# A fused attention and mixture-of-experts block: the last four batches of phase one in an order of their own, padding rows written during the steps, gates chosen in the expert stage

## The reference

```python
h = _layernorm(x) * (1 + ca) + sa
x = x + ga * attention(h)      # linear attention: 16 heads of 8, cumulative sums over the 256 tokens
h = _layernorm(x) * (1 + cb) + sb
x = x + gb * ffn(h)
# ffn: h = rmsnorm(h @ W_in.T); logits = h @ Wr.T; the best 2 of 8 experts by logits + bias
#      gates = softmax of the two chosen logits
#      expert e: rmsnorm((silu(h @ Wg[e].T) * (h @ Wu[e].T)) @ Wd[e].T)   (512 hidden)
#      out = sum of gates * expert outputs; rmsnorm(out) @ W_out.T
```

## Time and profile before

| | |
|---|---|
| median of 3 runs | 432.0 us (431.47, 432.0, 436.98) |
| profiled execution | 440.27 us, of which the span of the profile is 438.4 us |
| granted TensorE clock over the span | 0.931 of full |
| busy share of the span | PE 84%, DVE 77%, ACT 66%, POOL 57% |
| phase one, steps with all stages | about 30 to 180 us |
| drain, table, first loads | about 180 to 228 us |
| expert stage | about 228 to 398 us |
| last stage | about 403 to 438 us |

### The profile page before, as it was taken

The page is one execution under the profiler, slowest core; times in us unless marked ns, Lnnn a source line. Parts: engine busy times, 40 slices in busy tenths (PEclk is TensorE's granted clock), DMA queues, the critical chain, the costliest instruction groups (busy, mean ns, idle before and its releaser), DMA issues.

```text
span 438.4 us, 13203 instructions
## 1 busy us (share of the span) xinstructions
PE 366.1 (84%) x3906; PEld 321.1 (73%) x3907; DVE 338.8 (77%) x1113; ACT 290.9 (66%) x814; POOL 249.9 (57%) x221
## 2 busy tenths in 40 slices
PE   4799999979999999873129999999999999991464
PEld 3588878768888888762118999999999999981353
DVE  5077898869999998665599887878788788781586
ACT  4425768867888887534427776877768587773585
POOL 2964476668888888833532545456455554555341
PEclk9989999999999999985559999999999999998588
DMA  8994000000000000000141222122221222112933
GB/s 252 428 356 190 2 18 20 20 21 26 24 27 28 24 30 24 32 26 24 50 151 38 61 64 72 48 72 56 64 68 53 66 54 73 37 38 63 372 85 96
DMA packets 19107, 35.67 MB, mean 81 GB/s; under 512 B 3843, under 2 KB 14614, under 8 KB 18294
## 3 DMA queue, kind: packets, MB, share of 16 engines
q1 hardware_dynamic: 14262, 21.20, 15.4%
q0 software_dynamic: 4544, 9.39, 6.4%
q10 hardware_dynamic: 272, 4.72, 2.8%
HBM read 23.80 MB, written 13.47 MB: 85 GB/s over the span
## 4 chain that ended last, share of the span: by engine, by line
PE 56%; DVE 19%; issue 10%; DMA 7%; ACT 3%; POOL 3%; DVEq 1%; another core or an unknown queue 0%; ACTq 0%; SPq 0%; POOLq 0%
PE bank L1518 8%; PE bank L1520 8%; PE bank L1519 8%; PE bank L1335 6%; DVE prod L890 5%; PE bank L1533 4%; PE bank L1535 4%; PE bank L1534 4%; DMA gates_bc<-gate_rows 3%; PE bank L1504 2%; PE bank L1417 2%; DVE st L813 2%; PE bank L1444 1%; ACT junk L782 1%; DVE x_all L1085 1%
## 5 line engine op out<-in xcount | busy, mean ns | idle before, releaser
L543 POOL DMA_INDIRECT expert_rows<-late,to_place x78 | 86.7, 1111 | 83.2 <-DVE late L1191 56.8
L524 POOL DMA_INDIRECT dispatched<-rows,pos x64 | 67.1, 1049 | 38.0 <-issue 19.1
L1518 PE MATMUL bank<-late,w_hi 128*128 128x256 f16 x312 | 85.8, 275 | 1.5 <-issue 0.6
L1519 PE MATMUL bank<-late,w_hi 128*128 128x256 f16 x312 | 85.6, 274 | 0.0
L1520 PE MATMUL bank<-late,w_lo 128*128 128x256 f16 x312 | 85.6, 274 | 0.0
L506 POOL TENSOR_TENSOR kv<-kv,v 128x1024 f32<-128x1024 f32 x32 | 67.6, 2132 | 21.6 <-ACT kv L643 14.8
L1335 PE MATMUL bank<-cst,kv 128*128 128x128 f32 x576 | 77.0, 286 | 1.2 <-POOL kv L506 1.0
L1335 PEld LDWEIGHTS bank<-cst,kv 128*128 128x128 f32 x576 | 72.0, 201 | 1.9 <-POOL kv L506 1.1
L1180 DVE SCALAR_TENSOR_TENSOR kv<-bank,uscale,kv 128x512 f32<-128x512 f32 x78 | 58.0, 746 | 19.2 <-ACT kv L729 13.9
L729 ACT ACTIVATE kv<-bank,descale 128x512 f32<-128x512 f32 x78 | 53.5, 687 | 27.6 <-PE bank L1520 26.8
L735 ACT ACTIVATE kv<-kv 128x512 f16<-128x512 f32 x78 | 49.2, 631 | 20.5 <-DVE kv L1180 18.6
(11 more groups left out here) (212 smaller groups left out, 797.1 us busy)
## 6 DMA issues: line engine op xcount, KB each, us to landing
late<-dispatched SPq DMA_DIRECT2D x39, 129.0 KB
late<-wguT ACTq DMA_DIRECT2D x1, 4096.0 KB, 15.8
late<-expert_rows SPq DMA_DIRECT2D x1, 2064.0 KB, 11.2
gates_bc<-gate_rows SPq DMA_DIRECT2D x1, 2048.0 KB, 15.1
wd<-wdT SPq DMA_DIRECT2D x1, 2048.0 KB, 23.8
out<-kv SPq DMA_DIRECT2D x16, 128.0 KB, 1.8
expert_rows<-late,to_place POOLq DMA_INDIRECT x78
late<-expert_rows SPq DMA_DIRECT2D x1, 1032.0 KB, 6.8
```

Of the source, the lines that this page charges most:

```text
L524: pool.indirect_dma_start(hbuf, bass.IndirectOffsetOnAxis(ap=pos[:, p, t * K + k:t * K + k + 1], axis=0), rows[:, p, t, k, :], None).then_ ...
L543: pool.indirect_dma_start(ybuf, bass.IndirectOffsetOnAxis(ap=to_place[:, s, r:r + 1], axis=0), yt[:, s, r, :], None).then_inc(y_scat[s], 16)
L1518: mm(o, w_hi[:, w], hi, start=True, stop=False)
L1519: mm(o, w_hi[:, w], lo, start=False, stop=False)
```

## The change

Three things are changed.

1. Steps 17 to 20 are replaced by a `drain` function on PE, DVE, ACT and POOL, with an order of its own on each engine. To let batches overlap, odd batches use another PSUM bank (`UL_ODD` in KV's bank) for the expert features, ranks of b13 to b15 go to `LAST_RANK`, logits no longer wait for ACT's upper half, and ACT's upper half waits for the logits (`lr_done`). The scales of the down weights are computed in 6 DVE instructions in place of 9.
2. The filler rows are written in phase one: SP issues 17 DMAs of 2048 rows of 516 bytes (256 rows in each of the 8 regions), the whole of `dispatched`, two in flight. `positions` on DVE waits until the filler under the rows that the batch can reach has landed. The eight DMAs after the last batch, and `tail`, go.
3. The choice of the gates' logits moves from before L1148 into the third tile of the expert stage, and ACT's sigmoids to the end of that stage.

```diff
-            for s in range(B, B + 5):
-                step(*(at(s - g) for g in stages))
+            step(*(at(B - g) for g in stages))
+            drain(*(at(B - 4 + g) for g in range(4)))
...
-            sp.wait_ge(tail_done, 1)
...
-                sp.dma_start(hbuf[bass.ds(row, R), :], filler[e * R:(e + 1) * R, :]).then_inc(filled, 16)
+            sp.wait_ge(x_rest, 48)
+            sp.wait_ge(moe_ld, 32)
+            regions = hbuf[0:E * REGION, :].rearrange("(e r) w -> r e w", e=E)
+            padding = filler[0:E * R, :].rearrange("(e r) w -> r e w", e=E)
+            for s in range(REGION // R):
+                if s >= 2:
+                    sp.wait_ge(padded[s % 2], 16 * (s // 2))
+                sp.dma_start(regions[s * R:(s + 1) * R], padding).then_inc(padded[s % 2], 16)
...
             def positions(b, p, n):
                 dve.wait_ge(ohs_done, b + 1)
+                dve.wait_ge(padded[p], 16 * n)
...
# ScalarE
+            def drain(b12, b13, b14, b15):
+                last_rows(*b12)
+                spread(*b14)
+                turned_back(*b14)
+                second_turned(*b13)
...
+                squares(*b13, UL_ODD)
+                second_deviation(*b14)
+                last_rows(*b13)
+                spread(*b15)
+                second_norm(*b14)
...
# VectorE
+            def choice(b, p, n):
+                ul = UL_ODD if p else UL
+                dve.wait_ge(rms_done, b + 1)
+                nc.vector.reciprocal(rrs[:, p, :], rms[:, p, :]).then_inc(rrs_done, 1)
+                dve.wait_ge(rrs_done, b + 1)
+                logits(b, p, ul if b > B - 4 else UL)
+                scores(b, p, ebias[:])
...
+            def drain(b12, b13, b14, b15):
...
+                choice(*b13)
+                second_inverse(*b14)
+                second_shift(*b14)
+                denominators(*b15)
+                best_two(*b13)
+                rows_low(*b13)
+                slots_of(*b13)
+                quotients(*b15)
+                count_chosen(*b13[0:2])
+                add_attention(*b15)
+                choice(*b14)
+                second_inverse(*b15)
+                second_shift(*b15)
+                best_two(*b14)
+                rows_low(*b14)
+                slots_of(*b14)
+                count_chosen(*b14[0:2])
+                projection_scales()
+                choice(*b15)
+                best_two(*b15)
+                rows_low(*b15)
+                slots_of(*b15)
+                count_chosen(*b15[0:2])
...
-            then(nc.vector.tensor_tensor(tail_f[:], total[0:1, :], cst[0:1, C_REG:C_REG + E], ALU.add))
-            nc.vector.tensor_copy(tail[:], tail_f[:]).then_inc(tail_done, 1)
+            then(nc.vector.tensor_copy(total[:], TOTAL))
...
                     low_part(t, s, i, 0)
+                    if first and s == 2:
+                        choose_gates()
...
# TensorE
+            def drain(b12, b13, b14, b15):
+                running_state(b15, 0, False)
...
+                spread(*b14)
+                turn(*b13)
+                running_state(b15, 1, False, range(1))
+                ranks(*b12)
+                running_state(b15, 1, False, range(1, 3))
+                head_sums(b15, 0)
+                project(*b14)
+                into_experts(*b13)
+                head_sums(b15, 1)
+                spread(*b15)
+                ranks(*b13)
+                turn(*b14)
+                into_experts(*b14)
+                project(*b15)
+                ranks(*b14)
+                turn(*b15)
+                into_experts(*b15)
+                ranks(*b15)
```

More of the change, by code:

```diff
@@ L526, in step, with drain @@
                                 rows[:, p, t, k, :], None).then_inc(scattered[p], 16)
-            pipelined(pool, step)
+            def drain(*batches):
+                for rte in batches:
+                    step(None, None, None, None, None, rte)
+            pipelined(pool, step, drain)
             pool.wait_ge(w_small, 2)
@@ L587, in norm, with rows_high @@
                 last.then_inc(done, 1)
+            def rows_high(b, p, n, ul=UL):
+                if again(n):
+                    act.wait_ge(scattered[p], 16 * NT * K * (n - 1))
+                nc.scalar.activation(rows[:, p, :, :, D:HW].rearrange("p t k o -> p (t k) o"),
+                                     place_sb[:, bass.ds(b * NT * K, NT * K)].unsqueeze(2), ACT.Copy)
+                for t in range(NT):
+                    last = nc.scalar.activation(
+                        rows16[:, p, t, :, 0:D], ul[:, t, 0:D].unsqueeze(1).to_broadcast([P, K, D]),
+                        ACT.Copy, scale=rrs[:, p, t:t + 1])
+                last.then_inc(hi_done, 1)
@@ new lines, in squares @@
+            def squares(b, p, n, ul=UL):
+                act.wait_ge(u_ps, b + 1)
+                for t in range(NT):
+                    last = nc.scalar.activation(junk[:], ul[:, t, 0:D], ACT.Square, accum_out=ssq[:, p, t:t + 1])
+                    last.then_inc(ssq_done, 1)
+                    act.wait_ge(ssq_done, NT * b + t + 1)
+                nc.scalar.activation(rms[:, p, :], ssq[:, p, :], ACT.Sqrt, bias=eps_rms_h[:],
+                                     scale=1.0 / D / HSCALE ** 2).then_inc(rms_done, 1)
@@ L601, in step @@
-                    last.then_inc(hi_done, 1)
+                    act.wait_ge(rrs_done, rte[0] + 1)
+                    rows_high(*rte)
                 if prj is not None:
[L603 to L606, removed]
+                    spread(*prj)
                 if nrm is not None:
@@ L704, in projection_high @@
                                      scale=wd_by[:]).then_inc(wdhi_done, 1)
[L706 to L708 removed]
+            pipelined(act, step, drain)
+            for c in range(DN):
                 projection_high(c)
[L712 to L722 removed]
             def gate(t, s, i, h):
@@ L1483, in _ @@
+            pipelined(pe, step, drain)
             pe.wait_ge(count_done, B)
-            mm(bk[0][:, 0:E], ones16[:], oh_all[:, B, NT * K, :], start=True, stop=True).then_inc(total_ps, 1)
+            mm(TOTAL, ones16[:], oh_all[:, B, NT * K, :], start=True, stop=True).then_inc(total_ps, 1)
             pe.wait_ge(table_done, 1)
```

292 lines of the change are left out of this document (185 added, 107 removed).

## The result

The changed kernel is slower: 468.3 us (median of 4 runs, 464.2 to 473.3) against 434.0 (431.5 to 437.0) for the kernel before beside it, a ratio of 1.076 with a 95% interval of 1.063 to 1.088. The run of 473.3 was in a slower state, with a lower granted clock, and isn't in the ratio. Its profiled execution took 464.2 us, with a span of 462.1.

What follows compares the result with a forecast made beforehand. PE was taken to be full outside the drain and handover. Drain 7.7 plus gates and landing 1.7 less added waits 0.5 made 8.9 us, off the median of 432.0: 423.1 us, range 419 to 430.5 (forecast's own 420.5 to 426).

Steps and rivals of the forecast that it cites:

- What bounds the kernel: PE bounds the expert stage, PE and DVE phase one's full steps; only the 46.8 us of drain and handover can shorten.
- Part 1, the drain: In the last batches, the new order brings b15's positions at 207.6 against 215.33, a gain of 7.7 us.
- The mishap of 1.2 us: In the drain, 1.2 us allowed for one unexplained stop like the old drain's pair of transpositions.
- Part 2, the filler: Phase one's 17 filler DMAs, in by 106 us, add 0.5 us of DVE waits; the last scatter gains 2.06 us.
- I take 4 us, nearest to the first: Phase one: time per filler DMA, chosen between 3.2 us from the scatters' queue and 13.4 us.
- upper bound: Phase one: 13.4 us per filler DMA, from 1024 pieces of 512 bytes that took 6.7 us to land.
- Cost: nothing on the path; it is hidden in DMA engines that are 12% busy.: Phase one: the filler transfers cost nothing on the path; only the added DVE wait costs, 0.5 us.
- The last scatter lands in 2.3 us: Behind the last batch, without fillers beside it, the last scatter lands in 2.3 us; before, 4.35.
- Part 3, the gates: Handover to the experts: moving the gates' choice gives 1.7 us; first product 11.2 to 11.6 us after `pos`.
- Filler too slow: Phase one: b15's positions wait for fillers, slower than before from about 11.2 us per DMA, 467 at 13.4; chance 0.06.
- The clock falls early: In the drain, PE's low clock comes early and costs 3 to 4 us more; gain about 5, 427 us; chance 0.18.
- The change doesn't do what it says: In the drain, batches stay bound by each other's DVE work; gain 3, 429 us; chance 0.12.

Runs made afterwards that it cites:

- old_fill: The changed kernel with the padding written as before, after the last batch's positions, none in the steps; 426.2 against 432.9 us, ratio 0.985.
- gates_alone: The kernel before with only the gates' choice and the two sigmoids moved into the expert stage; 435.2 us, ratio 1.0035.
- eight_rows: The changed kernel with eight buffers for `rows` instead of two, fillers still in rows of 516 bytes; 437.4 against 433.8 us, ratio 1.008.
- fill_alone: The kernel before with the padding written in the steps (17 transfers, rows of 516 bytes), old order and gates; 481.8 us, ratio 1.110.
- long_alone: The kernel before, old order and gates, with the padding in the steps in pieces of 16 rows; 439.2 against 438.2 us, ratio 1.001.
- long16_chip2: The changed kernel with fillers in pieces of 16 rows, timed again beside other kernels on one chip; 425.5 against 433.8 us, ratio 0.982.
- long16: The changed kernel with the same fillers in pieces of 16 rows (8256 bytes); 425.6 against 432.9 us, ratio 0.983.
- one_in_flight: The changed kernel with one filler transfer outstanding instead of two, still in rows of 516 bytes; one run, 480.0 us.
- four_rows: The changed kernel with four buffers for rows and positions instead of two, and phase one's 16 steps written out; 456.1 against 438.2 us, ratio 1.041.

## Why the prediction was wrong

**What bounds the kernel** held: the expert stage took 174.3 us from first product to the loads, before 175.0.

**Part 1, the drain: right in the order's gain, too long at both ends.** The forecast had PE's start to b15's positions fall from 33.6 to 25.8 us. The changed kernel has 31.6 (209.21 to 240.78), 5.6 of it the stop of PE that the fillers caused, and PE's products run slower behind it (six cumulative sums take 1.49 us, 0.83 in old_fill). In old_fill the stretch is 23.3, milestone by milestone: b13's features 7.0 us behind PE's start (6.7 forecast), b15's projection 13.4 (14.4), b15's features 19.5 (20.9). The old order in gates_alone, timed beside it, takes 31.0 and not 33.6: the profile on which the forecast rested has a stop of PE there, 2.12 us before b14's projection and not 0.94, and behind it 18 cumulative sums took 3.41 us and not 2.17. So the order saves 31.0 - 23.3 = 7.7 (from POOL's start 35.8 - 28.1, the same). That this is the forecast to the decimal is luck: both of its ends were some 2.5 us too long. It also means that some 2.5 of the 8.3 us by which that profiled execution was over the median did lie in the drain. The mishap of 1.2 us that I allowed for is real, but all or nothing: no stop in some runs, 2.9 us of DVE in others, with which PE's wait at b15's denominators grows from 1.45 to 4.44; where it strikes, only 35.7 - 32.9 = 2.8 of the 7.7 are left. What releases it stays open.

**Part 2, the filler: the failed step.** This part was wrong in size and in place. The size, "I take 4 us, nearest to the first": a filler DMA took 10.1 us, near the upper bound. The lower one came from q0's row, 6.4% of 16 engines for 18176 rows, 24.7 ns each. But that row says 4544 packets: GpSimd's queue packs four rows, 2066 bytes, into one, and 98.8 ns is the price of a packet. The fillers send each row as a packet of its own, and 128 packets for each engine at that price would have been 12.6 us, the other bound over again. Read rightly, two rows said about 13, and I took 4, because the queues are empty later; but 2048 packets fill them by themselves.
The place: "Cost: nothing on the path; it is hidden in DMA engines that are 12% busy." The fillers took no compute engine's time, but the 16 DMA engines', and something else goes through the same ones, by a queue of its own (q0): the scatters, whose landing frees the buffer that ACT's L599 waits for. With the fillers beside them they landed after 11 to 14 us, where the last, with none, took 2.27. I priced the wait that the change adds (`padded`, forecast 0.5 us; it did not show in the changed kernel) and not the wait that was there already and had slack. eight_rows shows it by itself: 1.076 with that wait, 1.008 without, the same fillers under both. Why a landing comes so late beside a full queue is a further question, and open (last section).
"The last scatter lands in 2.3 us": right, 2.27.

**Part 3, the gates: right in sum, wrong in cause.** The first product came 11.65 us behind the positions, forecast 11.2 to 11.6. But alone the gates' move gives nothing (13.98, ratio 1.0035), and the padding alone gives 12.3 (fill_alone and long_alone). With both it is 11.6 to 12.2 (11.61 in long16_chip2, 12.12 in long16), so what the gates add is between nothing and 0.7. As forecast, `put_places` and POOL's product end together, at 255.7.

**The rivals.** *Filler too slow* had 0.06, and had the culprit but not the mechanism: b15's positions did not wait for the padding. Positions waited for it only where the other wait was gone, in eight_rows (b13's, 0.97 us; b15's 4.62 are a scatter's), and where the fillers were slower, in one_in_flight (8.32). By that mechanism alone a c of 10.1 costs nothing, and that its 467 us lies beside the measured 468.3 is a coincidence. *The clock falls early*: from 230 us on it was halved in the changed kernel (0.50 to 250), as before (0.54). In the steps it fell to 0.93 with the stops and stayed at 1.00 in eight_rows beside the same fillers, so it is no cause of its own; what part of the loss it adds there wasn't measured. *The change doesn't do what it says*, that is, the new order doesn't pay: excluded by old_fill.

## What to carry to other kernels

Price a transfer that is to run "in the background" by its pieces, not its bytes, and then list everything else that goes through the same engines during it, with who waits for its landing and how much slack that wait has: here a landing could take about 7 us before anyone waited (from the last scatter's issue to L599 of two batches on, in four_rows's even steps), and it took 11 to 14. Once that wait is gone, look for the next: `pos` was a second double buffer behind the same scatters. Write long pieces (a DMA in runs of 16 rows took 3.8 us where single rows took 10.1), and price by packets where the page counts them. Parts that are timed only together hide each other: the new order was worth 1 to 2%, the fillers cost 9.

## What the runs showed of the hardware

- A packet of 516 bytes took a DMA engine 68 to 77 ns, from DRAM or from SBUF, one of 8256 bytes 408; GpSimd's scatters put four rows into a packet, for 98.8 ns, and 154 beside the fillers.
- With one filler DMA outstanding instead of two, a scatter beside it lands in 11.5 instead of 13.2 us, so it does not stand behind all that was handed over earlier. The Trainium skill (DMA: Bandwidth & Descriptors, "Queues, rings and completion order") says that an engine goes round its queues and drains a packet from one before it turns to the next; the small difference agrees. But taking turns doesn't explain the late landing. q0's 4544 packets are 32 for each of the 142 scatters, so a batch's four are 8 an engine; in turns with the fillers' packets they would land, as an estimate from the two measured times, 8 x (154 + 77) ns = 1.8 us later, and 9 to 12 us later was measured. Why a scatter lands so late is not shown.
- ACT and DVE stop for 0.8 to 5.4 us with no releaser in the profile. All eight profiles of two sets of kernels that ran side by side have such stops, and none of the eight of the other two sets; the medians of the kernel before in these sets were 439.8 and 438.2 against 432.9 and 433.8. The profile before has two, that of the changed kernel none. With packets of 516 or 2064 bytes there were five to nine of them, in the other four kernels two to five.
